# A decoder kernel: keys, values and queries of the first batch moved among the last chunks of the scan

## The reference

```
x = LN(x + mamba(x))       # 512 inner channels, 16 states, convolution over 4 tokens
x = LN(x + attention(x, context))   # 16 heads of 16
x = LN(x + experts(x))     # 4 experts, top 2, 256 -> 256 -> 256, each with two LNs

mamba: x_ssm, z = split(x @ W_in.T); x_ssm = silu(conv(x_ssm)); B, C, dt = x_ssm @ W_x.T
  h = exp(dt * A) * h + (x_ssm * dt) * B     # per channel and state, along the tokens
  y = sum_n(h * C) + x_ssm * D;  out = (y * silu(z)) @ W_out.T
attention: q, k, v with biases, softmax(q k / 4) v, @ Wo + bo
```

## Time and profile before

| | |
|---|---|
| three runs | 1559.48, 1568.10, 1569.07 us (median 1568.10) |
| the profiled execution | 1564.17 us, its span 1562.4 us |
| mean granted TensorE clock | 0.943 |
| busy | PE 1329.2 (85%), VectorE 1373.8 (88%), ScalarE 1107.8 (71%), GpSimd 1003.6 (64%) |
| DMA | 78.52 MB, mean 50 GB/s |
| first block | to 939.9 us; scans end at 892.7 |
| stage's load | issued by SyncE at 828.50 us, landed 5.5 us later |
| second block | from 940.2 us; batches 0 to 2 have a period of 157.15 us |

### The profile page before, as it was taken

The page is one execution under the profiler, slowest core; times in us unless marked ns, Lnnn a source line. Parts: engine busy times, 40 slices in busy tenths (PEclk is TensorE's granted clock), DMA queues, the critical chain, the costliest instruction groups (busy, mean ns, idle before and its releaser), DMA issues. The chain is left out here.

```text
span 1562.4 us, 22513 instructions
## 1 busy us (share of the span) xinstructions
PE 1329.2 (85%) x7506; PEld 935.2 (60%) x7506; DVE 1373.8 (88%) x2507; ACT 1107.8 (71%) x2539; POOL 1003.6 (64%) x702
## 2 busy tenths in 40 slices
PE   7788788878877887787777879999999999999997
PEld 5666666766766666676665552547354735473465
DVE  6999999999999999999999663678888888888798
ACT  5977988898889888988986515336833683368475
POOL 3999999999999999999999601100750075007401
PEclk9899989898999999999998978999999999999999
DMA  6202211220222022102202004100001000000000
GB/s 221 75 2 75 89 49 42 88 89 10 80 89 89 2 89 89 68 23 89 82 21 89 14 14 170 58 1 1 1 27 59 1 1 28 28 1 1 1 28 27
DMA packets 46646, 78.52 MB, mean 50 GB/s; under 512 B 3841, under 2 KB 40290, under 8 KB 42306
## 3 DMA queue, kind: packets, MB, share of 16 engines
q1 hardware_dynamic: 46530, 77.08, 14.8%
HBM read 68.16 MB, written 8.91 MB: 49 GB/s over the span
## 5 line engine op out<-in xcount | busy, mean ns | idle before, releaser
L974 POOL TENSOR_TENSOR state_c<-state,c_area 128x1024 f32<-128x1024 f32 x256 | 601.0, 2364 | 17.4 <-DVE state L1053 13.8
L1053 DVE TENSOR_TENSOR_SCAN state<-decay,ps 128x512 f32<-128x512 f32 x384 | 463.3, 1210 | 3.2 <-ACT decay L725 1.5
L725 ACT ACTIVATE decay<-step_area,negA 128x255 f32<-128x255 f32 x768 | 324.7, 497 | 0.0
L1809 POOL TENSOR_TENSOR big<-big,g_sb 128x1024 f32<-128x1024 f32 x27 | 71.3, 2641 | 384.6 <-ACT big L1663 368.2
L425 PE MATMUL ps<-ident_sb,state_c 128*128 128x128 f32 x2048 | 286.7, 291 | 0.7 <-POOL state_c L974 0.7
L425 PEld LDWEIGHTS ps<-ident_sb,state_c 128*128 128x128 f32 x2048 | 256.3, 152 | 19.6 <-issue 8.4
L1021 DVE TENSOR_TENSOR ps<-step_area,ps 128x512 f32<-128x512 f32 x384 | 261.4, 681 | 6.6 <-PE ps L409 4.9
L1053 DVE TENSOR_TENSOR_SCAN state<-ps,ub 128x512 f32<-128x512 f32 x128 | 154.7, 1208 | 15.8 <-ACT ps L738 9.9
L941 POOL TENSOR_TENSOR ub<-step_area,b_bc 128x1024 f32<-128x1024 f32 x64 | 151.7, 2371 | 25.6 <-DMA b_bc<-bc_scratch 25.6
L409 PE MATMUL ps<-parts,sel_bc_sb 96*128 96x256 bf16 x192 | 55.4, 289 | 101.4 <-DVE ps L1037 89.8
L1585 PE MATMUL ps<-w_sb,hT 128*128 128x256 f32 x512 | 118.7, 384 | 7.6 <-ACT ps L1689 5.1
(11 more groups left out here) (237 smaller groups left out, 2482.8 us busy)
## 6 DMA issues: line engine op xcount, KB each, us to landing
c_area<-bc_scratch SPq DMA_DIRECT2D x32, 1024.0 KB, 10.0
b_bc<-bc_scratch SPq DMA_DIRECT2D x16, 512.0 KB, 6.4
weights<-in_xT SPq DMA_DIRECT2D x16, 256.0 KB, 3.0
res<-in_x SPq DMA_DIRECT2D x16, 256.0 KB, 2.8
x_scratch<-res SPq DMA_DIRECT2D x16, 256.0 KB, 5.7
weights<-x_scratch SPq DMA_DIRECT2D x4, 1024.0 KB, 8.9
xa<-x_scratch SPq DMA_DIRECT2D x4, 1024.0 KB, 5.7
out_x<-acc SPq DMA_DIRECT2D x3, 1024.0 KB, 4.5
```

What stands on the lines that cost most here:

```text
L725: nc.scalar.activation(decay_tile(i, n)[:, j, 1:], dt_sb[:, i[1] % 2, j, 1:], ACT.Exp, scale=negA[:, j * NS + n:j * NS + n + 1]).then_inc( ...
L974: nc.gpsimd.tensor_tensor(state_c[:, n % RING, :, :], state[:, n % RING, :, :], c_bc[:, q, n, :].unsqueeze(1).to_broadcast([P, CT, TC]), A ...
L1053: nc.vector.tensor_tensor_scan(state[:, n % RING, pair, :].rearrange("p j n -> p (j n)"), a, b, 0.0, ALU.mult, ALU.add).then_inc(s_scan, 1)
```

## The change

- Own buffers for kT, kTr, v and v_rem. In their place in `weights` lies acc, the accumulator of the second block.
- keys(0), keys(1), values(False) and values(True) are issued in slot 10 of turns 11, 12, 13 and 14, and taken by ScalarE in slot 12. y_back of these turns waits for that.
- The last turn has the contexts in slots 0 to 3 of TensorE (taken in 4 to 7), queries 0 to 5 in slots 4 to 9 (taken in 8 to 13), queries 6 and 7 in slots 14 and 15 (taken behind the turns). All queries use w_ps.
- The clears of kTr and v_rem move from the last turn to GpSimd's start.
- Second block: gate_exp behind evict(1) and preset(TT + 3) in all batches; the measure of tile 6 behind the last rounds in batches 0 to 2; GpSimd's last gain waits for all eight x2 tiles in every batch; in batch 3 the order is bias(8), four measures, aggregate, bias(2), weigh, bias(22).

```diff
+        KV_AT = NCH - 5
+        QUERIES = 6
...
                     if not more:
                         pe.wait_ge(s_r, at(k, CTT, 2 * CTT))
-                        pe.wait_ge(s_qc, G + 1 + 2 * (k[1] - NCH + 2))
-                    if k[1] == NCH - 3:
-                        pe.wait_ge(s_kp, 2)
+                        pe.wait_ge(s_qc, QUERIES + 2 * (k[1] - NCH + 2))
+                    job = k[1] + 1 - KV_AT
+                    if 0 <= job < 2:
+                        pe.wait_ge(s_kp, 2 * job + 2)
+                    elif 2 <= job < 4:
+                        pe.wait_ge(s_kvc, 2 + HG * (job - 2))
...
                 if u == 0:
                     pe.wait_ge(s_stage, 16)
-                    pe.wait_ge(s_kp, G)
+                    pe.wait_ge(s_r, CTT * NCH)
...
-                    pe.wait_ge(s_dt, CT * NCH)
-                else:
-                    pe.wait_ge(s_r, CTT * NCH)
+                pe.wait_ge(s_dt, CT * (KV_AT + h + 2))
...
                 if v == 0:
-                    pe.wait_ge(s_kvc, 6)
+                    pe.wait_ge(s_xtc, NL * KT)
                 else:
                     pe.wait_ge(s_qc, v)
-                if v == G + 1:
+                if v == QUERIES:
                     pe.wait_ge(s_r, ALL_SUMS - CTT)
...
             def values(rem):
 
+                pe.wait_ge(s_dt, CT * (KV_AT + (5 if rem else 4)))
...
-                if i[1] == NCH - 2:
-                    work += [(10, lambda: keys(0))]
+                job = i[1] - KV_AT
+                if 0 <= job < 2:
+                    work += [(10, lambda: keys(job))]
+                elif 2 <= job < 4:
+                    work += [(10, lambda: values(job == 3))]
                 if i[1] == NCH - 1:
-                    work += [(0, lambda: keys(1)), (1, lambda: context(0)), (2, lambda: context(1)), (3, lambda: context(2)),
-                             (4, lambda: context(3)), (5, lambda: values(False)), (6, lambda: values(True))]
-                    work += [(7 + max(v - 1, 0), lambda v=v: query(v)) for v in range(G + 1)]
-                    work += [(14, lambda: query(G + 1)), (15, lambda: query(G + 2))]
+                    work += [(u, lambda u=u: context(u)) for u in range(NL * KT)]
+                    work += [(4 + v, lambda v=v: query(v)) for v in range(QUERIES)]
+                    work += [(8 + v, lambda v=v: query(v)) for v in range(QUERIES, NL * G)]
...
             add_state(last, NS - 2)
-            query(G + 3)
             round_max(1)
...
                 if i[1] == NCH - 1:
-                    work += [(4, lambda: take_keys(1)), (5, lambda: take_context(0)), (5, lambda: take_context(1)),
-                             (6, lambda: take_context(2)), (7, lambda: take_context(3)), (8, lambda: take_values(False)),
-                             (9, lambda: take_values(True))]
-                    work += [(10 + max(v - 1, 0), lambda v=v: take_query(v)) for v in range(G + 1)]
+                    work += [(4 + u, lambda u=u: take_context(u)) for u in range(NL * KT)]
+                    work += [(8 + v, lambda v=v: take_query(v)) for v in range(QUERIES)]
...
                         preset(TT + 2)
-                        if more:
-                            gate_exp(b)
...
-                        if t == 1 and not more:
+                        if t == 1:
                             gate_exp(b)
...
                     if more and t == TT - 1:
-                        pool.wait_ge(s_x2, (b + 1) * TT + (TT if b + 1 == LAST else 1))
+                        pool.wait_ge(s_x2, (b + 1) * TT + TT)
...
-                    if t:
+                    if t and (t < TT - 1 or not more):
                         measure(b, (t - 1) // TG, (t - 1) % TG, s_l1c)
...
                 while work:
                     advance(2 * TT)
+                if more:
+                    measure(b, 1, TG - 2, s_l1c)
                 measure(b, 1, TG - 1, s_l1c)
...
-                    bias(10)
-                    for i in range(TG - 1):
+                    bias(8)
+                    for i in range(TG):
                         measure(b, 0, i, s_l2c)
-                    bias(6)
-                    measure(b, 0, TG - 1, s_l2c)
                     aggregate(b, 2 + NT)
-                    bias(4)
+                    bias(2)
                     weigh(b, 0)
-                    bias(12)
+                    bias(22)
```

More of the change, by code:

```diff
@@ L461, in query @@
                 if v == 0:
-                    pe.wait_ge(s_kvc, 6)
+                    pe.wait_ge(s_xtc, NL * KT)
                 else:
                     pe.wait_ge(s_qc, v)
-                if v == G + 1:
+                if v == QUERIES:
                     pe.wait_ge(s_r, ALL_SUMS - CTT)
                 for c in range(KT):
-                    last = nc.tensor.matmul(ps[:, 7 if v < G + 3 else 4, :], w["wq"][:, c, g * P:(g + 1) * P],
+                    last = nc.tensor.matmul(w_ps[:, :], w["wq"][:, c, g * P:(g + 1) * P],
                                             x1T[:, c, half * HALF:(half + 1) * HALF], start=c == 0, stop=c == KT - 1)
@@ L472, in values @@
             def values(rem):
+                pe.wait_ge(s_dt, CT * (KV_AT + (5 if rem else 4)))
                 if not rem:
                     pe.wait_ge(s_ones, 1)
-                    pe.wait_ge(s_xtc, NL * KT)
                     for c in range(KT):
@@ L480, in values @@
                     return
-                pe.wait_ge(s_kvc, 2)
                 for j in range(HG):
@@ L781, in take_query @@
                     act.wait_ge(s_sc, RING + (NCH - 1) * NS)
-                nc.scalar.activation(qT[:, g, half * HALF:(half + 1) * HALF], ps[:, 7 if v < G + 3 else 4, :], ACT.Identity,
+                nc.scalar.activation(qT[:, g, half * HALF:(half + 1) * HALF], w_ps[:, :], ACT.Identity,
                                      scale=HD ** -0.5, bias=w["bqk"][:, g:g + 1]).then_inc(s_qc, 1)
@@ L795, in turn @@
                              (13, lambda: next_lead(k))]
-                if i[1] == NCH - 2:
-                    work.append((12, lambda: take_keys(0)))
+                job = i[1] - KV_AT
+                if 0 <= job < 2:
+                    work.append((12, lambda: take_keys(job)))
+                elif 2 <= job < 4:
+                    work.append((12, lambda: take_values(job == 3)))
                 if finish:
@@ L854, in _ @@
                 take_sum(shift(last, -1), t)
-            take_query(G + 1)
-            take_query(G + 2)
+            for v in range(QUERIES, NL * G):
+                take_query(v)
             spreads(shift(last, -1))
-            take_query(G + 3)
             guess(shift(last, -1))
@@ L967, in turn @@
                 if i[1] == NCH - 1:
-                    work += [(1, lambda: clear(kTr)), (2, lambda: clear(v_rem)), (6, lambda: clear(neg[0]))]
+                    work += [(6, lambda: clear(neg[0]))]
                 for n in range(NS):
@@ L985, in _ @@
             pool.sem_inc(s_norm, CTT)
+            clear(kTr)
+            clear(v_rem)
             first, last = (None, 0), (None, NCH - 1)
@@ L1212, in attn_ffn_block @@
         wsum = sb("wsum", [P, TT])
-        acc = sb("acc", [P, TT, DM])
+        acc = late["acc"]
         scale2 = sb("scale2", [P, NT, TG * E])
@@ L2230, in decoder_block @@
                          views(weights, (TAPS, CT, P), (KT, DI), (KT, DI), (2, KT, TC), (CT, HALO + TC), (CT, PROJ))))
-        late = dict(zip(("stage", "x1T", "kT", "kTr", "v", "v_rem"),
-                        views(weights, (TT, DM), (KT, L), (G, S), (G, P), (NH, BLK), (G, P))))
+        late = dict(zip(("stage", "x1T", "acc"), views(weights, (TT, DM), (KT, L), (TT, DM))))
+        for name, shape in (("kT", (G, S)), ("kTr", (G, P)), ("v", (NH, BLK)), ("v_rem", (G, P))):
+            late[name] = ctx.enter_context(nc.sbuf_tensor(name + "_sb", [P, *shape], F32))
         late["ctx"] = ctx.enter_context(nc.sbuf_tensor("ctx_sb", [P, KT, S], F32))
```

## The result

The changed kernel takes 1568.5 us (median of 20 runs), the kernel before 1564.1 (20 runs too). The ratio is 1.003, its 95% interval 1.0016 to 1.0043: some 4.4 us slower, forecast +3.1. The profiled executions say less: 1564.17 us before and 1565.03 after, 0.86 apart. That is not what the medians say, and the experiments show where most of the difference lies. ("before" and "after" are the two kernels; e1 to e11 are further kernels, each made of one of these by a small edit.

The account below looks back on a forecast made before the run. VectorE's pace was taken to bound the first block's recurrence. Jobs +13.5, last chunk with tail -3.0 and second block -7.4 gave +3.1 on 1568.1, so 1571 us, range 1557 to 1583.

Parts of the forecast that it names:

- Turns 11 and 12: First block, one keys job in each turn: 2.97 us each, 5.9 us slower together.
- Turn 13: First block, values(False): take_y_back at T + 6.55, 4.98 us late; T is the start of the table load after terms.
- Turn 14: First block, values(True) replacing keys: take_y_back at T + 7.15, 5.6 us late (bounds 4.2 and 7.8), net +2.6.
- The last chunk: End of the first block: 6.8 us of waits go, 4.8 come, -2.0; VectorE's take_y 0.5 later.
- The tail: Behind the last chunk: query(7) no longer stands between the first two rounds of maxima, -1.0 us.
- Block 2: The second block's edits together: -7.4 us, bounds -4 and -9.
- three prices: Second block, per batch: gate_exp -1.28 and measure -0.45 in three batches, GpSimd's wait -1.10 in two.
- Batch 3 reorder 0: Second block, batch 3's new order: ScalarE's wait of 2.54 us goes, but the end hangs on VectorE's sum, so 0.
- the boundary: Rival: out_tile(1) makes VectorE pay up to 3.5 us at each of four turn boundaries, 1585 us; chance 0.12.
- keep its clock: Rival: TensorE keeps full clock through slots 10 to 12 of the job turns, -6.5, 1564.5 us; chance 0.13.
- The jobs hide: Rival: ScalarE catches up within the turn, turns 11 to 14 cost some 3 us, not 13.5; 1560.7 us; chance 0.17.
- ScalarE has no slack: First block, slot 12: VectorE pays a keys job's whole 2.97 us, its gaps having grown by 2.87.

Follow-up runs that it names:

- e1: The kernel after with the second block's four edits taken back, so only the first block is changed: 1576.4 us, ratio 1.0084.
- e11: e9 with the last turn's out_tile(0) and (1) in slots 13 and 14 and queries 6 and 7 in slot 15: 1550.0 us, ratio 0.9917.
- e3: The kernel after with the four jobs moved from TensorE's slot 10 to 7 and ScalarE's takes from slot 12 to 10: 1555.1 us, ratio 0.9945.
- e4: The kernel after with seven zero-adding matmuls ahead of the job in slot 10 of turns 11 to 14: 1564.9 us, ratio 0.9991.
- e6: The kernel before with only GpSimd's last gain waiting for all eight x2 tiles in batches 0 and 1: batch distances 157.36 and 157.35 us (one run).
- e8: e3 with take_context(3) in ScalarE's slot 6 of the last turn instead of slot 7: 1554.9 us, ratio 0.9948.
- e9: e8 with four zero-adding matmuls in TensorE's slot 10 of every turn that prepares a next one: 1551.2 us, ratio 0.9929.
- e5: The kernel before with only gate_exp moved behind evict(1) and preset(TT + 3) in batches 0 to 2: batch distances 155.77 and 155.76 us (one run).
- e7: The kernel before with only the tile 6 measure move and batch 3's new order: batch distances 156.70 and 156.68 us, batch 3's newt to end 71.70 (one run).

## Why the prediction was right, and where not

The sum holds by its parts: by kernels of their own the first block costs +12.1 us (forecast 13.5 - 3.0 = +10.5) and the second gives -7.7 (forecast -7.4). Within the parts some misses cancel.

- **Turns 11 and 12**: right to 0.2 in sum, and that by luck. Turn 11 costs 1.8 and turn 12 4.0, for 2.97 each. I took the usual gap of 0.21 from turn 13; but in before turn 11 already has gaps of 0.63 and 0.93 and turn 12 one of 1.02, part of which the jobs' gaps swallow. In turn 12 the gaps behind ScalarE are 3.7 and not 3, and the gap of 1.08 ahead of the product for n = 13, which I had not seen, comes on top.
- **Turn 13**: right to 0.3 (T + 6.28 for T + 6.55). The matmuls at the lower clock took 4.7 us, estimated 4.46.
- **Turn 14**: the term that was furthest off. "With the first 3.5 us at the half clock I take 5.0": the granted clock was 0.51 over the whole group, and values(True) took 6.1 us. y_back came at T + 9.06 and not T + 7.15. I had taken the 3.58 us of the last chunk, where the group came behind other matmuls. The bound of 7.8 late covered it (9.06 - 1.57 = 7.5). Of the 1.9 us more, 1.3 showed in the turn.
- **The last chunk**: each of the three new or kept waits is there with its cause: query(0) behind a 6.15 us pause took 3.78 (taken: 3.34), b_row(11) 1.35, b_row(15) 4.02. -1.8 for -2.5.
- **The tail**: -1.0 was forecast. Round 1's wait fell from 1.97 to 0.93, by 1.04, as said; the other 1.6 in this profile is clock. Like with like the tail is -1.0 in executions with a good clock there and -0.2 in the others (e1).
- **Block 2**: gate_exp, measure and the GpSimd wait as forecast when together, -2.97 for -2.83. Right by half luck: I added three prices, and one of them is worth nothing without the others. "Batch 3 reorder 0" was +0.36: ScalarE's 2.54 were not on the path, and VectorE now waits 0.26 for the rstd, which four bias steps used to cover. GpSimd's two gains there took 6.83 us for 5.41, while the 22 bias steps stayed at 0.40 each. A gain takes 2.36 alone; beside bias steps it is longer by about as long as they still run (two gains from 1531.25, steps to 1533.47: 2.2 us of overlap, 2.1 longer). So GpSimd loses even to steps that are issued after its gain has started, against the rule of the Trainium skill (SBUF — State Buffer, Who interferes with whom) that the first to issue blocks the other.
- **Rivals**: the boundary did not break (out_tile(1) 3.67 us at 665.15, no gap of VectorE there). TensorE did not keep its clock (0.60 and 0.50 behind terms). "The jobs hide" is false in ScalarE's slot 12 and, by e3, nearly true in its slot 10. The Trainium skill (TensorE: Matmul & The Clock Gate, Part 1: The HAM clock gate) has the throttled clock as the default that activity releases; e4, in which filling the pause brings values(True) from 6.1 to 3.6 us, agrees with it.

What I had not asked is whether another slot would do. The cost of the jobs was nearly right and "ScalarE has no slack" the wrong reason: by e3 and e4 most of it is not ScalarE's work, but the wait for TensorE inside ScalarE's chain.

## What to carry to other kernels

A job that makes a round trip between engines costs what the chain-setting engine waits inside it, not what it works: put the producer under something that engine does anyway (here a table load), and take the result later. Before a removed wait is counted, look at what TensorE's clock does behind the next wait of TensorE; and compare two profiles stretch by stretch with the granted clock beside it, or a lucky execution hides 5 us. Where TensorE must stand in every iteration, matmuls that add zero can pay.

## What was not expected

- TensorE's wait of 1.76 us is followed by a granted 1.00 in before and 0.69 in e6, which only came to it 1.15 us earlier in its batch; alike in both batches that the edit reaches (distances of 157.36 and 157.35).
- The eight tensor_scalars beside GpSimd's gain take 0.83 us each, without it 0.33.
- Four added matmuls (1.8 us) in each of 15 turns, 27 us of TensorE's time, made the kernel faster by 3.7 us in the medians of e8 and e9, with overlapping intervals of the ratio; VectorE's waits in the two traces differ by about 4 us.
- Up to the start of turn 11 all kernels but e9 and e11 run the same code, but for two clears of GpSimd; take_y of turn 11 starts between 622.3 and 626.6 us in their profiles. What differs most are waits of VectorE for which the profile gives no releaser: before take_y (0.4 to 2.2 us in all), and in e5 and e7 once 3.3 and 3.2 us before a product.
- The runs of after spread from 1564.9 to 1575.7, with the mean granted clock falling from 0.941 to 0.928 as the time rises.
